# Attention scores of batches 1 to 7 as three fp32r products instead of one fp32 product

## The chip, the cores and the metric

The kernel runs on one core of one Trainium2 chip. Its time is the device time of one execution in microseconds; the figure for the kernel before is the median of three runs. The engines that matter here are TensorE (PE, with PEld for its weight loads), VectorE (DVE), ScalarE (ACT) and GpSimd (POOL). Each works through its own instructions in the order of the program and waits on semaphores that the others count up.

## The reference, cut to what matters

```python
x = x + attn(layernorm(x))          # x: 8 batches of 512 rows of 128
x = x + ffn(layernorm(x))           # 16 experts, the best 4 of each row
x = x + ssm(layernorm(x))
x = x + ffn(layernorm(x))

def attn(x):                        # one batch
    q, k, v = split(x @ w_qkv.T)
    scores = (q @ k.T) / sqrt(8)
    return softmax(scores) @ v @ w_proj.T + b_proj
```

The kernel folds the two projections of the scores into one matrix: `a_qk` is Wq^T Wk / sqrt(8), so with xn the normalised rows the scores are (xn a_qk) xn^T. What the kernel calls q is xn a_qk, and the other operand of the scores is xn itself.

## The kernel before

All four engines run an order that is written out by hand. The attention stage treats one batch per step, `step(i, ...)` for i from -1 to 7, and in step i three batches are in work at once: the softmax and output of batch i, the normalisation, the transposed rows `xnT` and the q of batch i+1, and the router (which experts a row goes to) of batches i-1 and i-2. Batch i has 512 rows, held as 4 groups r of 128 rows. The two sides of the buffers `xnT`, `qT` and `v` take turns by batch.

In a step from 2 to 6 the work goes round like this. Names in brackets are tiles, as the rows of the profile name them, with the line of the kernel before.

- PE: `scores(i, 0)`, `scores(i, 1)` (L1569), `router_turn(i-2)` (L1626, transposes of the router's rows `t0`), `scores(i, 2)`, `project(i-1)` (L1617), `scores(i, 3)`, `p_turn(i, 0)` and `p_turn(i, 1)` (L1599, transposes of the probabilities), `xn_turn(i+1)` (L1579), `router_logits`, `pv(i, 0)` (L1609), `q_proj(i+1)` (L1584), `p_turn(i, 2)`, `v_proj`, `p_turn(i, 3)`, the rest of `pv`, `router_parts`.
- ACT: `router_t` (L659 into tT, then L661 into ffn_hi), `exps(i, 0)` and `exps(i, 1)` (L623, probs), `pT` (L629), `xnT_out(i+1)` (L636), `exps(i, 2)`, `exps(i, 3)`, `q_out(i+1)` (L641), and later the rest of `pT`, `router_exp` (L666), `attn_out`, `v_out`.
- DVE: statistics of batch i+1 (L1050, L1053), `maxes(i, 0)` and `maxes(i, 1)` (L1065, neg_max), `xn_out(i+1)` (L1059), `maxes(i, 2)`, `x1_out` (L1075), the router's statistics of batch i-1 (L1081, L1084), `maxes(i, 3)`, the router's choice for batch i-2 (L1103 to L1140, of which L1128 waits for ACT's exponentials), and last `router_norm(i-1)` (L1090, four tensor_scalar instructions into t0) and `router_xn(i-1)` (L1096).
- POOL: `ln1_chain(i+1)` (L460, L462), `add_bias(i+1)` (L468), `router_stash(i-2)` (L454, the low part of the router's rows, a subtraction of 128x512), and `router_chain(i-1)` (L434 and L449, nine small instructions, each of which waits for the one before it). `router_norm(i-1)` on DVE waits for the ninth.

The score product of one group of rows in fp32 is one matmul in the program; the trace shows two records for it. The FFN stages that follow already hold their operands as a high part (a copy in fp32r) and a low part (the fp32 value less the high part), and form each product in three passes. After the last attention step POOL also splits the first rows of routing weights in step 7 (`rows_split`, L476 and L478), directly behind the router's chain of step 6.

Of the kernel before, what the change touches and what calls it, by code (L numbers as in the profile page):

```python
# [39 lines left out]
def build(nc, x, w_qkv, w_proj, b_proj, W_in, conv_w, conv_b, dt_bias, A_log, Dskip, norm_w, W_out,  # L40
          ffn_scale, gate_w, gate_b, mlp1_w, mlp1_b, mlp2_w, mlp2_b, out):
    with ExitStack() as ctx:
# [82 lines left out]
        with ExitStack() as stage:  # L125
            def own(name, shape, dt=F32):
                return stage.enter_context(nc.sbuf_tensor(name, shape, dt))


            w2_rows = own("w2_rows", [P, NE, I])  # L130
            w1_rows = own("w1_rows", [P, NE, D])
            xnT = own("xnT", [P, 2, SEQ])
            qT = own("qT", [P, 2, SEQ])
            probs = own("probs", [P, NT, SEQ])
            probsT = own("probsT", [P, NT, NT, P])
            v = own("v", [P, 2, NT, D])
            attn = own("attn", [P, NT, D])
            neg_max = own("neg_max", [P, NT])
            row_sum = own("row_sum", [P, NT])
            row_rec = own("row_rec", [P, NT])  # L140
            proj_rows = own("proj_rows", [P, D])
            qkv_rows = own("qkv_rows", [P, 3, D])

            tap_rows = w1_rows.rearrange("p (k w) d -> p k w d", w=CONV_W)
        with ExitStack() as stage:
# [42 lines left out]
        def bank(i):  # L188
            return ps[:, i, :]
# [29 lines left out]
        gate_b_all = vecs[:, VG:VG + NE]  # L219

        S1 = {n: sem("attn_" + n) for n in (
            "stats", "aggr", "rstd", "xn", "xnT_ps", "xnT", "q_ps", "q", "v_ps", "v", "scores", "max", "probs",
            "pT_ps", "pT", "o_ps", "rec", "o", "y_ps", "xb", "x1")}

        def router_sems(tag):
# [166 lines left out]
        def _(eng):  # L392
# [77 lines left out]

            eng.wait_ge(consts, N_CONST)

            def rows_split(F):
                b = 0
                wait(eng, rows_in, 48 * (b + done(F) + 1))
# [14 lines left out]
            def step(i, odd, first, second, third, fourth):  # L490
                if not first:
                    rows_split(F1)
                if first:
                    ln1_chain(i + 1)
                    add_bias(i + 1)
                if fourth:
                    router_stash(R1, i - 2)
                if third:
                    router_chain(R1, i - 1)
            skewed(eng, step, before={1: lambda: (late_constants(), ssm_weights()), 2: b2_parts})  # L500

            def ssm_norm(b):
# [104 lines left out]
        def _(eng):  # L607
# [30 lines left out]
            def q_out(b, par):  # L638
                wait(eng, S1["q_ps"], b + 1)
                wait(eng, S1["scores"], NT * (b - 1))  # L640
                eng.activation(qT[:, par, :], bank(4), ACT.Copy).then_inc(S1["q"], 1)  # L641

            def v_out(b, par):
                wait(eng, S1["v_ps"], b + 1)
# [205 lines left out]
            def step(i, odd, first, second, third, fourth):  # L850
# [26 lines left out]
                    pT(i, 1)  # L877
                if first:
                    xnT_out(i + 1, 1 - odd)
                if second:  # L880
                    exps(i, 2)
                if first:
# [160 lines left out]
        def _(eng):  # L1043
# [18 lines left out]
            def maxes(b, r):  # L1062
                wait(eng, S1["scores"], NT * b + r + 1)
                wait(eng, S1["probs"], NT * (b - 1) + r + 1)
                eng.tensor_reduce(neg_max[:, r:r + 1], bank(r), AX.X, ALU.max, negate=True).then_inc(S1["max"], 1)  # L1065

            def recip(b):
                wait(eng, S1["probs"], NT * b + NT)
# [296 lines left out]
            def step(i, odd, first, second, third, fourth):  # L1365
# [27 lines left out]
                    prep(i + 1, 3)  # L1393
                if fourth:
                    router_top(R1, i - 2)
                if second:
                    recip(i)
                if fourth:
# [151 lines left out]
        def _(eng):  # L1550
# [13 lines left out]
            def scores(b, par, r):  # L1564
                if (b, r) == (0, 0):
                    eng.wait_ge(prep_sb, 3)
                wait(eng, S1["q"], b + 1)
                wait(eng, S1["pT"], NT * (b - 1) + r + 1)
                eng.matmul(bank(r), qT[:, par, r * P:(r + 1) * P], xnT[:, par, :], start=True,  # L1569
                           stop=True).then_inc(S1["scores"], 1)  # L1570

            def xn_turn(b):
                if b:
                    wait(eng, S1["xn"], NT * b + NT)
                wait(eng, S1["q"], b)
                for r in range(NT):
                    if b == 0:
                        eng.wait_ge(S1["xn"], r + 1)
# [549 lines left out]
```

## Time and profile before

| | |
|---|---|
| median of three runs | 724.89 us (724.85 to 726.3) |
| the profiled execution, its own time | 726.56 us |
| span of the profiled execution | 724.8 us |
| PE busy over the span | 98% |
| DVE, ACT, POOL busy | 86%, 79%, 34% |
| attention steps 2 to 6, start of `scores(i, 0)` | 44.26, 57.57, 70.89, 84.20, 97.52 us |

The span is the time from the first to the last instruction that the profiler recorded. Busy shares are averages over stages; the change touches the attention stage alone, roughly the first 125 us.

### The profile page before, as it was taken

Reading aid. Unit: us, or ns where it says so; the run is one execution under the profiler, and the core shown is the slowest. Engines: PE = TensorE matmul, PEld = TensorE weight load, DVE = VectorE, ACT = ScalarE, POOL = GpSimd, SP = SyncE. Lnnn points to the kernel's source line nnn. Section 1 sums busy time; section 2 is a strip of 40 time slices with the busy share of each in tenths; the row PEclk is TensorE's granted clock in tenths of the full one; section 3 lists DMA queues with packets and bytes.
Section 4 is the critical chain, followed back from the end, with each engine's and each line's share of the span. In section 5 each row is a group of like instructions: output and inputs, shape, how many; then the busy total and the mean of one; then the engine's idle time right before and its main releaser. Section 6 shows DMA issues by size and latency. Waiting matters only on the chain.

```text
span 724.8 us, 13089 instructions
## 1 busy us (share of the span) xinstructions
PE 711.4 (98%) x3826; PEld 580.4 (80%) x3826; DVE 625.4 (86%) x1503; ACT 574.8 (79%) x1097; POOL 242.9 (34%) x389
## 2 busy tenths in 40 slices
PE   8999999999999999999999999999999999999998
PEld 6788787888788877778888888888878887887886
DVE  3678886999999999967689899899889989898996
ACT  2776767988988899778787787777678889888885
POOL 2454564000015100015757767767760000610000
PEclk9999999999999999999999999999999999999999
DMA  9000002654555454300000000000055455555651
GB/s 264 16 2 3 12 30 91 224 191 158 182 189 187 163 172 182 141 0 2 1 1 1 4 3 1 9 4 1 33 202 194 171 194 201 200 189 169 223 198 52
DMA packets 29380, 77.19 MB, mean 106 GB/s; under 512 B 4899, under 2 KB 9726, under 8 KB 29310
## 3 DMA queue, kind: packets, MB, share of 16 engines
q1 hardware_dynamic: 28980, 76.29, 30.9%
q8 instruction: 31, 0.51, 0.3%
q14 instruction: 39, 0.32, 0.1%
q10 hardware_dynamic: 330, 0.08, 0.0%
HBM read 73.73 MB, written 2.62 MB: 105 GB/s over the span
## 4 chain that ended last, share of the span: by engine, by line
PE 49%; DVE 2%; issue 1%; POOL 1%; ACT 1%; DVEq 0%; POOLq 0%; ACTq 0%
PE ps L1701 4%; PE ps L1703 4%; PE ps L1702 4%; PE ps L1733 4%; PE ps L1734 4%; PE ps L1735 4%; PE ps L1950 3%; PE ps L1755 3%; PE ps L1756 3%; PE ps L1757 3%; PE ps L1973 2%; PE ps L2008 2%; PE ps L1959 2%; PE ps L1985 1%; PE ps L1965 1%
## 5 line engine op out<-in xcount | busy, mean ns | idle before, releaser
L712 ACT ACTIVATE s_ring<-ps,b1T 128x512 f32<-128x512 f32 x256 | 171.3, 687 | 35.9 <-PE ps L1735 34.6
L1183 DVE SCALAR_TENSOR_TENSOR s_ring<-s_ring,top_col,r_all 128x1024 f32<-128x1024 f32 x128 | 166.3, 1300 | 19.2 <-ACT s_ring L712 18.4
L1195 DVE TENSOR_TENSOR s_lo<-s_ring,s_hi 128x1024 fp32r<-128x1024 f32 x126 | 153.6, 1219 | 1.9 <-ACT s_hi L718 1.9
L718 ACT ACTIVATE s_hi<-s_ring 128x1024 fp32r<-128x1024 f32 x128 | 135.0, 1055 | 9.9 <-DVE s_ring L1183 8.9
L1701 PE MATMUL ps<-s_hi,w_hi 128*128 128x512 f32 x256 | 101.7, 397 | 2.6 <-DVE s_lo L1195 2.5
L1733 PE MATMUL ps<-ffn_hi,w_hi 128*128 128x512 f32 x256 | 103.7, 405 | 0.2 <-ACT s_ring L712 0.2
L1703 PE MATMUL ps<-s_hi,w_lo 128*128 128x512 f32 x256 | 101.3, 396 | 0.0
L1735 PE MATMUL ps<-ffn_hi,w_lo 128*128 128x512 f32 x256 | 101.2, 395 | 0.0
L1734 PE MATMUL ps<-ffn_lo,w_hi 128*128 128x512 f32 x256 | 101.1, 395 | 0.0
L1702 PE MATMUL ps<-s_lo,w_hi 128*128 128x512 f32 x256 | 100.9, 394 | 0.0
L1701 PEld LDWEIGHTS ps<-s_hi,w_hi 128*128 128x128 f32 x256 | 48.2, 188 | 17.0 <-DVE s_lo L1195 6.2
L527 POOL TENSOR_TENSOR ramp<-upto,dt_a 128x512 f32<-128x512 f32 x32 | 33.0, 1041 | 85.4 <-PE ps L1703 73.8
L1702 PEld LDWEIGHTS ps<-s_lo,w_hi 128*128 128x128 f32 x256 | 48.2, 188 | 11.1
L1735 PEld LDWEIGHTS ps<-ffn_hi,w_lo 128*128 128x128 f32 x256 | 48.0, 188 | 11.3
L1703 PEld LDWEIGHTS ps<-s_hi,w_lo 128*128 128x128 f32 x256 | 48.2, 188 | 11.0
L1733 PEld LDWEIGHTS ps<-ffn_hi,w_hi 128*128 128x128 f32 x256 | 48.2, 188 | 10.7 <-ACT s_ring L712 0.7
L1734 PEld LDWEIGHTS ps<-ffn_lo,w_hi 128*128 128x128 f32 x256 | 48.2, 188 | 9.7
L454 POOL TENSOR_TENSOR ffn_lo<-tT,ffn_hi 128x512 fp32r<-128x512 f32 x16 | 22.5, 1404 | 88.8 <-ACT ffn_hi L661 88.8
L434 POOL TENSOR_TENSOR rt_small<-rt_small,mhalf 128x4 f32<-128x4 f32 x32 | 37.8, 1181 | 2.5
L1260 DVE SCALAR_TENSOR_TENSOR conv_acc<-ps,conv_taps,conv_acc 128x511 f32<-128x511 f32 (+2 forms) x48 | 35.0, 742 | 1.4 <-ACT conv_acc L769 1.3
L434 POOL TENSOR_TENSOR rt_small<-rt_mv,eps 128x4 f32<-128x4 f32 x16 | 7.7, 480 | 81.2 <-DVE rt_mv L1084 80.5
L1973 PEld LDWEIGHTS ps<-xb_tok,gram 128*128 128x128 f32 x256 | 32.9, 192 | 1.9 <-issue 0.5
(267 smaller groups left out, 1559.4 us busy)
## 6 DMA issues: line engine op xcount, KB each, us to landing
r_all<-route_dram SPq DMA_DIRECT2D x128, 512.0 KB, 3.9
out_dram<-X SPq DMA_DIRECT2D x7, 256.0 KB, 4.3
X<-in_L_attn_a_x_dram SPq DMA_DIRECT2D x1, 1536.0 KB, 8.6
rows_f<-route_dram SPq DMA_DIRECT2D x48, 32.0 KB, 3.0
w_rows<-in_L_ffn_mlp_w_dram SPq DMA_DIRECT2D x1, 1024.0 KB, 7.9
route_dram<-route_cols SPq DMA_DIRECT2D x64, 8.0 KB, 1.5
X<-in_L_attn_a_x_dram SPq DMA_DIRECT2D x2, 256.0 KB, 5.5
ssm_rows<-in_L_attn_b_W_in_dram SPq DMA_DIRECT2D x1, 384.0 KB
```

The lines of the kernel that those rows point to most:

```text
L434: eng.tensor_tensor(o, a, bb, op).then_inc(R["pool"], 1)
L712: eng.activation(s_ring[q % NR][:, e % 2, :], h_bank(F, b, e), ACT.Silu, bias=b1T[:, e:e + 1], scale=ALPHA).then_inc(F["act"], 1)
L718: eng.activation(s_hi[q % NR][:, :, :], s_ring[q % NR][:, :, :], ACT.Copy).then_inc(F["hi"], 1)
L1183: eng.scalar_tensor_tensor(out=s_ring[q % NR][:, :, :], in0=s_ring[q % NR][:, :, :], scalar=top_col[:, 0:1], in1=r_all[q % NR][:, :, :], o ...
L1195: eng.tensor_tensor(s_lo[q % NR][:, :, :], s_ring[q % NR][:, :, :], s_hi[q % NR][:, :, :].bitcast(F32), ALU.subtract).then_inc(F["lo"], 1)
L1701: eng.matmul(bank(6), w2_hi[:, e, :], hi, start=False, stop=False)
L1702: eng.matmul(bank(6), w2_hi[:, e, :], lo, start=False, stop=False)
L1703: mm = eng.matmul(bank(6), w2_lo[:, e, :], hi, start=False, stop=(e == NE - 1))
L1733: eng.matmul(h_bank(F, b, e), w1_hi[:, e, :], ffn_hi[:, b, :], start=True, stop=False)
L1734: eng.matmul(h_bank(F, b, e), w1_hi[:, e, :], ffn_lo[:, b, :], start=False, stop=False)
L1735: eng.matmul(h_bank(F, b, e), w1_lo[:, e, :], ffn_hi[:, b, :], start=False, stop=True).then_inc(F["h"], 1)
L1973: mm = eng.matmul(bank(3)[:, h * HD:(h + 1) * HD], gram[:, c % 2, h, :], xb_tok[:, c % 2, h // 2, (h % 2) * HD:(h % 2 + 1) * HD], start=Fa ...
```

## The change

From batch 1 on, the score product uses three fp32r passes: high q by high rows, low q by high rows, high q by low rows. Batch 0 keeps the fp32 product, with its q in a tile of its own. Four things are new in every step from 0 to 6, for batch i+1: on ACT `xnT_high` copies xnT into `xnT_hi`, between `xnT_out` and `exps(i, 2)`; on POOL `xnT_low` subtracts to get `xnT_lo`, between `add_bias` and the router's chain; on DVE `q_low` subtracts `qT` (now fp32r) from q's bank to get `qT_lo`, ahead of `recip`; and PE waits for the three of them. On POOL the two router pieces also change places: `router_chain` now stands ahead of `router_stash`.

```diff
-            qT = own("qT", [P, 2, SEQ])
+            qT = own("qT", [P, 2, SEQ], F32R)
...
+            xnT_hi = own("xnT_hi", [P, 2, SEQ], F32R)
+            xnT_lo = own("xnT_lo", [P, 2, SEQ], F32R)
+            qT_lo = own("qT_lo", [P, 2, SEQ], F32R)
+            q_first = own("q_first", [P, SEQ])
...
+            def xnT_low(b, par):
+                wait(eng, S1["xnT_hi"], b)
+                wait(eng, S1["scores"], NT * (b - 1))
+                eng.tensor_tensor(xnT_lo[:, par, :], xnT[:, par, :], xnT_hi[:, par, :].bitcast(F32),
+                                  ALU.subtract).then_inc(S1["xnT_lo"], 1)
...
                 if first:
                     ln1_chain(i + 1)
                     add_bias(i + 1)
+                if first and second:
+                    xnT_low(i + 1, 1 - odd)
+                if third:
+                    router_chain(R1, i - 1)
                 if fourth:
                     router_stash(R1, i - 2)
-                if third:
-                    router_chain(R1, i - 1)
...
-                eng.activation(qT[:, par, :], bank(4), ACT.Copy).then_inc(S1["q"], 1)
+                out = q_first[:, :] if b == 0 else qT[:, par, :]
+                eng.activation(out, bank(4), ACT.Copy).then_inc(S1["q"], 1)
+
+            def xnT_high(b, par):
+                wait(eng, S1["xnT"], b + 1)
+                wait(eng, S1["scores"], NT * (b - 1))
+                eng.activation(xnT_hi[:, par, :], xnT[:, par, :], ACT.Copy).then_inc(S1["xnT_hi"], 1)
...
                     xnT_out(i + 1, 1 - odd)
+                    xnT_high(i + 1, 1 - odd)
                 if second:
                     exps(i, 2)
...
+            def q_low(b, par):
+                wait(eng, S1["q"], b + 1)
+                wait(eng, S1["scores"], NT * (b - 1))
+                eng.tensor_tensor(qT_lo[:, par, :], bank(4), qT[:, par, :].bitcast(F32), ALU.subtract).then_inc(S1["q_lo"], 1)
...
                     router_top(R1, i - 2)
+                if first and second:
+                    q_low(i + 1, 1 - odd)
                 if second:
                     recip(i)
...
-                eng.matmul(bank(r), qT[:, par, r * P:(r + 1) * P], xnT[:, par, :], start=True,
-                           stop=True).then_inc(S1["scores"], 1)
+                rows = slice(r * P, (r + 1) * P)
+                if b == 0:
+                    eng.matmul(bank(r), q_first[:, rows], xnT[:, par, :], start=True,
+                               stop=True).then_inc(S1["scores"], 1)
+                    return
+                wait(eng, S1["xnT_hi"], b)
+                eng.matmul(bank(r), qT[:, par, rows], xnT_hi[:, par, :], start=True, stop=False)
+                wait(eng, S1["q_lo"], b)
+                eng.matmul(bank(r), qT_lo[:, par, rows], xnT_hi[:, par, :], start=False, stop=False)
+                wait(eng, S1["xnT_lo"], b)
+                eng.matmul(bank(r), qT[:, par, rows], xnT_lo[:, par, :], start=False, stop=True).then_inc(S1["scores"], 1)
```

POOL's rows in one step from 2 to 6, in the kernel before (`ln_ve` and `ln_rs` are the normalisation of the attention, `rt_small` is the router's chain, `ffn_lo` the stash):

```order
L460 TENSOR_TENSOR ln_ve<-ln_mv,eps 128x4
L462 TENSOR_TENSOR ln_rs<-ln_ve,mhalf 128x4
L468 TENSOR_TENSOR X<-X,vecs 128x512
L454 TENSOR_TENSOR ffn_lo<-tT,ffn_hi 128x512
L434 TENSOR_TENSOR rt_small<-rt_mv,eps 128x4
...
L434 TENSOR_TENSOR rt_small<-rt_small,ones 128x4
L449 TENSOR_TENSOR rt_small<-rt_small,rt_mv 128x4
```

The same step in the changed kernel:

```order
L464 TENSOR_TENSOR ln_ve<-ln_mv,eps 128x4
L466 TENSOR_TENSOR ln_rs<-ln_ve,mhalf 128x4
L472 TENSOR_TENSOR X<-X,vecs 128x512
L480 TENSOR_TENSOR xnT_lo<-xnT,xnT_hi 128x512
L438 TENSOR_TENSOR rt_small<-rt_mv,eps 128x4
...
L438 TENSOR_TENSOR rt_small<-rt_small,ones 128x4
L453 TENSOR_TENSOR rt_small<-rt_small,rt_mv 128x4
L458 TENSOR_TENSOR ffn_lo<-tT,ffn_hi 128x512
```

The new subtraction stands where the stash stood, and the stash now stands behind the ninth instruction of the chain.

ACT's rows from `router_t` to `q_out` in the same step, before:

```order
L659 ACTIVATE tT<-ps,scale_col 128x512
L661 ACTIVATE ffn_hi<-tT 128x512
L623 ACTIVATE probs,row_sum<-ps,neg_max 128x512 x2
L629 ACTIVATE probsT<-ps 128x512 x2
L636 ACTIVATE xnT<-ps 128x512
L623 ACTIVATE probs,row_sum<-ps,neg_max 128x512 x2
L641 ACTIVATE qT<-ps 128x512
```

And in the changed kernel:

```order
L677 ACTIVATE tT<-ps,scale_col 128x512
L679 ACTIVATE ffn_hi<-tT 128x512
L635 ACTIVATE probs,row_sum<-ps,neg_max 128x512 x2
L641 ACTIVATE probsT<-ps 128x512 x2
L648 ACTIVATE xnT<-ps 128x512
L659 ACTIVATE xnT_hi<-xnT 128x512
L635 ACTIVATE probs,row_sum<-ps,neg_max 128x512 x2
L654 ACTIVATE qT<-ps 128x512
```

One copy is added, between `xnT_out` and the third group's exponentials.

## Rows read from the trace of the kernel before

**Rows 1.** The page, part 1: busy time of each engine, share, instructions.

```profile
PE 711.4 (98%) x3826; PEld 580.4 (80%) x3826; DVE 625.4 (86%) x1503; ACT 574.8 (79%) x1097; POOL 242.9 (34%) x389
```

**Rows 2.** Busy time by stretch, step 5: length, engines, granted clock, DMA.

```profile
84.20:97.52 13.32, 13.32 (x94) 10.73 (x93) 11.25 (x56) 9.18 (x23) 7.20 (x13) 1.00 0.15 51
```

**Rows 3.** Timeline of PE, steps 5 and 6: start, length, what, count.

```profile
86.36 1.02 PE L1569 MATMUL ps<-xnT,qT 128*128 128x512 f32 x2
87.22 1.05 PE L1617 MATMUL ps<-vpg,attn 128*128 128x128 f32 x8
...
99.67 1.02 PE L1569 MATMUL ps<-xnT,qT 128*128 128x512 f32 x2
```

**Rows 4.** Timeline of PE, step 7: six fp32r passes between fp32 work.

```profile
118.31 0.48 PE L1733 MATMUL ps<-ffn_hi,w_hi 128*128 128x512 f32 x1
...
119.79 1.04 PE L1599 MATMUL ps<-ident,probs 128*128 128x128 f32 x8
```

**Rows 5.** Timeline of DVE, steps 4 and 5.

```profile
83.37 1.11 DVE L1090 TENSOR_SCALAR t<-X,rt_mv,rt_small 128x128 f32<-128x128 f32 x4
...
86.97 1.25 DVE L1065 TENSOR_REDUCE neg_max<-ps 128x1 f32<-128x512 f32 x2
...
92.22 0.66 DVE L1065 TENSOR_REDUCE neg_max<-ps 128x1 f32<-128x512 f32 x1
...
95.78 0.24 DVE L1128 TENSOR_TENSOR rt_tmp<-rt_tmp 128x64 f32<-128x64 f32 x1 [0.90 <-ACT rt_tmp L666]
```

**Rows 6.** Timeline of ACT, step 5.

```profile
86.56 0.69 ACT L659 ACTIVATE tT<-ps,scale_col 128x512 f32<-128x512 f32 x1 [0.42 <-PE ps L1626]
87.36 0.63 ACT L661 ACTIVATE ffn_hi<-tT 128x512 fp32r<-128x512 f32 x1
87.90 0.67 ACT L623 ACTIVATE probs<-ps,neg_max 128x512 f32<-128x512 f32 x1
...
89.61 1.08 ACT L629 ACTIVATE probsT<-ps 128x512 f32<-128x512 f32 x2 [0.28 <-PE ps L1599]
90.58 0.60 ACT L636 ACTIVATE xnT<-ps 128x512 f32<-128x512 f32 x1
```

**Rows 7.** Timeline of POOL, step 5.

```profile
89.74 1.28 POOL L468 TENSOR_TENSOR X<-X,vecs 128x512 f32<-128x512 f32 x1 [1.33 <-DVE xn L1059]
90.98 1.27 POOL L454 TENSOR_TENSOR ffn_lo<-tT,ffn_hi 128x512 fp32r<-128x512 f32 x1
92.38 0.20 POOL L434 TENSOR_TENSOR rt_small<-rt_mv,eps 128x4 f32<-128x4 f32 x1
...
96.30 0.20 POOL L449 TENSOR_TENSOR rt_small<-rt_small,rt_mv 128x4 f32<-128x4 f32 x1
```

**Rows 8.** Timeline of POOL, end of step 6 and start of step 7.

```profile
109.59 0.20 POOL L449 TENSOR_TENSOR rt_small<-rt_small,rt_mv 128x4 f32<-128x4 f32 x1
109.72 0.61 POOL L476 CAST rows_r<-rows_f 80x512 fp32r<-80x512 f32 x1
110.41 1.27 POOL L478 TENSOR_TENSOR rows_r<-rows_f,rows_r 16x512 fp32r<-16x512 f32 x1
114.90 1.27 POOL L454 TENSOR_TENSOR ffn_lo<-tT,ffn_hi 128x512 fp32r<-128x512 f32 x1 [3.22 <-ACT ffn_hi L661]
```

**Rows 9.** Timeline of DVE, end of step 6; the last row is instructions 2 to 4.

```profile
110.33 2.20 DVE L1090 TENSOR_SCALAR t<-X,rt_mv,rt_small 128x128 f32<-128x128 f32 x4
...
111.69 0.85 DVE L1090 TENSOR_SCALAR t<-X,rt_mv,rt_small 128x128 f32<-128x128 f32 x3
```

**Rows 10.** Timeline of ACT, start of step 7.

```profile
114.09 0.63 ACT L661 ACTIVATE ffn_hi<-tT 128x512 fp32r<-128x512 f32 x1
114.63 0.67 ACT L623 ACTIVATE probs<-ps,neg_max 128x512 f32<-128x512 f32 x1
```

**Rows 11.** Timelines of ACT and POOL, step 1.

```profile
37.21 0.60 ACT L636 ACTIVATE xnT<-ps 128x512 f32<-128x512 f32 x1
...
38.94 0.20 POOL L434 TENSOR_TENSOR rt_small<-rt_mv,eps 128x4 f32<-128x4 f32 x1 [3.07 <-DVE rt_mv L1084]
```

More of the change, by code:

```diff
@@ L221, in build @@
         S1 = {n: sem("attn_" + n) for n in (
-            "stats", "aggr", "rstd", "xn", "xnT_ps", "xnT", "q_ps", "q", "v_ps", "v", "scores", "max", "probs",
+            "stats", "aggr", "rstd", "xn", "xnT_ps", "xnT", "xnT_hi", "xnT_lo", "q_ps", "q", "q_lo", "v_ps", "v", "scores", "max", "probs",
             "pT_ps", "pT", "o_ps", "rec", "o", "y_ps", "xb", "x1")}
@@ L1575, in xn_turn @@
                 wait(eng, S1["q"], b)
+                wait(eng, S1["q_lo"], b - 1)
                 for r in range(NT):
```

## The prediction

> **What bounds the kernel now.** I read the page first: PE is busy 98% of the span, DVE 86%, ACT 79%, POOL 34% [rows 1]. Then the stretches: a step of the attention stage takes 13.32 us, PE is busy in all of it at a granted clock of 1.00, and DVE has 11.25 us of work, ACT 9.18, POOL 7.20 [rows 2]. The five steps from 2 to 6 start 13.31 us apart, and the timeline of PE shows the same place one step later at 99.67 - 86.36 = 13.31 us [rows 3]. So PE sets the step, and time taken from PE comes out of the end, as long as nothing else is nearly as late. That is the question here, since everything the change adds lies on the other three. The timelines of DVE, ACT and POOL [rows 5 to 7] show a ring that runs through them and closes once a step, almost as long as PE's step:
>
> `router_norm` (DVE, 83.37) - `router_xn` and the statistics - `maxes(i, 0)` (86.97) - `exps(i, 0)` (ACT, 87.90) - `pT` - `xnT_out` (90.58). On the other side `router_stats` - `router_chain` on POOL (92.38 to 96.30 + 0.20) - `router_norm` of the next step (83.37 + 13.31 = 96.68), 0.18 us after the chain's end. In the kernel before, the first half and the second touch only through DVE's own order. The change ties them: `xnT_low` waits for ACT's copy of `xnT_out`, and the router's chain stands behind `xnT_low`.
>
> **What PE gains.** One fp32 score product takes 87.22 - 86.36 = 0.86 us [rows 3]. Six fp32r passes of the same 512 columns between fp32 work take 119.79 - 118.31 = 1.48 us, so three take 0.74 [rows 4]. Four groups give back 4 x 0.12 = 0.48 us a step, and PE then has 12.8 us of work. The weight loads of fp32r stay hidden in that row.
>
> **The ring after the change.** I count from E, the start of `exps(i, 0)`.
>
> - `xnT_out` starts at 90.58 - 87.90 = 2.68 and lasts 0.60, to 3.28 [rows 6]. PE's transposes between them wait for ACT's probabilities, so an earlier PE does not pull this in.
> - `xnT_high` is new. Its twin is L661, the same copy of 128x512 to fp32r: it starts 87.36 - (86.56 + 0.69) = 0.11 after the copy it reads and lasts 0.63 [rows 6]. End 4.02.
> - ACT to POOL: L454 starts at 114.90, and the copy it waits for ended at 114.09 + 0.63 = 114.72, so 0.18 [rows 8, 10]. `xnT_low` starts at 4.20.
> - `xnT_low` is the twin of the stash, 1.27 us [rows 7]. After such an instruction the next starts 90.98 - 89.74 = 1.24 behind its start [rows 7]: the chain starts at 5.44. Before it started at 92.38 - 87.90 = 4.48, so this is 0.96 later.
> - From the chain's first start to its last 96.30 - 92.38 = 3.92 [rows 7]: 9.36.
> - The stash now follows at once. What follows the ninth instruction directly starts 109.72 - 109.59 = 0.13 later [rows 8], so it runs from 9.49 to 10.76, just when `router_norm` is released at about 9.6.
> - Here the trace shows something that the order alone doesn't. In step 6 `router_norm` starts at 110.33, POOL's 512-column subtraction L478 at 110.41, and the four instructions take 2.20 us where they take 1.11 in step 4; numbers 2 to 4 start at 111.69, when L478 ends (110.41 + 1.27 = 111.68) [rows 5, 8, 9]. So DVE's tensor_scalar is held until POOL's long instruction has ended, and then needs 0.85 more [rows 9]. For the stash that gives an end of `router_norm` at 10.76 + 0.85 = 11.61. Unheld it takes 1.11, so the rest of DVE runs as if it had started at 10.50.
> - `router_norm` to `maxes(i+1, 0)` is DVE's own work without a gap: 86.97 - 83.37 = 3.60 [rows 5]. The maximum takes 0.66, and ACT starts some 0.04 later [rows 5]: E of the next step is 10.50 + 4.30 = 14.80.
>
> The step becomes 14.80 us in place of 13.31, **1.49 us longer**. PE's 0.48 us is then worth nothing. Without the hold `router_norm` would start at 9.36 + 0.20 + 0.03 = 9.59 and the step would be 13.89, 0.58 longer. The same sum for the kernel before is 4.48 + 3.92 + 0.23 + 4.30 = 12.93, so the ring has 0.38 us of slack now.
>
> The Trainium skill bears on the hold: "GPSIMD Engine Reference", section 8, says that GpSimd shares its SBUF interfaces with VectorE and contends with VectorE instructions in a 2-port perf mode or with two SBUF inputs. "VectorE: DVE Perf Modes", on mode 2x_2P, puts tensor_scalar from SBUF to SBUF there, in fp32 too. By that rule the stash and `router_norm` collide in every step; with no such rule the sum would be the one without the hold. The trace agrees with the rule in the step 6 collision, 2.20 us against 1.11 [rows 5, 9].
>
> **What else is added.** `q_low` reads one bank and one SBUF tile, like `neg_max` over a bank, 0.66 us [rows 5]. It falls in the 0.90 us that DVE idles for the router's exponentials ahead of L1128 [rows 5]. If that cover were gone it would cost up to 0.66 a step, but with POOL's chain later than before it has another microsecond. It also delays `recip`, which only `attn_out` needs, at the end of the step. `xnT_high` pushes `exps(i, 2)` by some 0.6 us; `exps(i, 3)` waits for its maximum anyway. The stash, one chain later, is needed by `router_t` of the next step, and ends before it. `xnT_low` runs beside statistics and maxima, as the stash did. No DMA moves. Step 0 has no chain and POOL and ACT idle there, so I count nothing.
>
> **The sum.**
>
> - Step 1: `xnT_low` starts at 37.21 + 0.60 + 0.11 + 0.63 + 0.18 = 38.73, the chain at 39.97 instead of 38.94 [rows 11]: 1.03 later. ACT's start of `exps` is 87.90 - (86.97 + 0.70) = 0.23 behind DVE's path in step 5 [rows 5, 6]; I take 0.3 of slack. **+0.7**
> - Steps 2 to 5: 4 x 1.49 = **+6.0**
> - Step 6: before, the hold was there already: `router_norm` ended at 111.69 + 0.85 = 112.54, which is 11.33 after E (87.90 + 13.31 = 101.21) [rows 6, 9]. Now the stash stands ahead of the two pieces of `rows_split`: stash start 9.49, L476 at 10.73, L478 0.69 behind it at 11.42, its end 12.69, `router_norm` ends at 13.54 [rows 7, 8]. **+2.2**, and +0.3 if DVE gets its four through ahead of them. In step 6 before POOL won with an instruction that came 0.08 us later, so I take 2.2.
> - Step 7 and after: E follows `router_norm` as before, 114.63 - 112.54 [rows 9, 10]; the FFN, the SSM and the second FFN move as a block. The stash in step 7 has nothing hurried behind it. **0**
>
> Together **+8.9 us**. The profiled execution took 726.56 us at a span of 724.8; its sum gives 735.5. The median of the runs is 1.67 us lower, so there I expect 724.89 + 8.9 = **733.8 us**. The case's own range, from a step 0.1 us shorter or 0.15 longer and from +0.3 in step 6: 731.5 to 735.
>
> **Rivals.**
>
> - *The hold doesn't come* (0.14): if DVE, once released, gets ahead of the stash or runs between its accesses. Against it: the stash has started some 0.1 us earlier. Then 0.7 + 4 x 0.58 + about 0.6 = 3.6, so 728.5 us.
> - *PE stays the bound* (0.10, the other side): if `xnT_low` gets its data before the router's statistics are there, the chain is not late. The point at which that decides is 0.38 us of slack against 0.96 of delay, so my reading of one link would have to be off by over half a microsecond. Then six steps bring 0.48 us each, 2.9 in all: 722.0 us.
> - *More is held* (0.08): `xnT_low` or the later chain also hold DVE's small two-input instructions, or `q_low` lands on the ring. With 0.66 more a step in four to six steps: 736.5 to 738 us.
> - *The change shows nothing* (0.04): the gain and the delay meet, because the ring loses only its slack. 724.9 us.
> - *PE's clock falls* (0.02): PE would idle 2 us of a 14.8 us step, and the rows have no such stretch at a steady pace. With 12.8 of 14.8 us of work it stands a granted clock down to 0.87 without loss; below that the price is open.
>
> **The numbers.** My case has 0.62. What a measurement of this kernel can tell from no change is about 0.2%, 1.45 us. Slower by more: 0.62 + 0.14 + 0.08 + 0.02, less a little where the rivals are small, 0.85; faster 0.10; same 0.05. The range takes in my case and the one without the hold and a little of the worse: 727.8 to 736.
>
> **What would show it.** In the changed kernel: steps 2 to 5 some 14.8 us apart; PE idle twice, ahead of `router_turn` (waiting for DVE's t0) and ahead of `p_turn(i, 0)` (waiting for probs); the chain on POOL starting when `xnT_low` ends, about 5.4 us after `exps(i, 0)`; the four of `router_norm` at some 2.3 us in steps 2 to 5 and over 3 in step 6; a score group at 0.70 to 0.78 us. I am wrong if PE is still without gaps, if `router_norm` takes 1.1 us beside the stash, or if the chain starts at its old distance.

## The result and the profile after

| | before | after |
|---|---|---|
| median of the runs taken together | 725.6 us (724.85 to 726.74, 4 runs) | 732.6 us (732.28 to 733.58, 4 runs) |
| profiled execution, its own time | 726.56 us | 732.87 us |
| span | 724.8 us | 731.1 us |
| step 5, start of `exps(5, 0)` to that of the next step | 13.31 us | 14.62 us |

The ratio is 1.01, with a 95% interval of 1.0081 to 1.012: the change makes the kernel **slower by 7.0 us**. I had expected 733.8 us and a loss of 8.9.

The page of the kernel after, its first part (the same line as [rows 1]):

```profile
PE 709.2 (97%) x3854; PEld 582.6 (80%) x3854; DVE 635.2 (87%) x1510; ACT 580.5 (79%) x1104; POOL 250.4 (34%) x396
```

PE has 2.2 us less busy time although it has 28 more instructions, and the span is 6.3 us longer. So PE now waits. The busy time by stretch for step 5 of the kernel after (length, busy time of PE, PEld, DVE, ACT and POOL, granted clock, DMA share and rate):

```profile
85.90:100.53 14.63, 13.33 (x99) 11.29 (x97) 12.92 (x56) 10.04 (x24) 8.44 (x15) 1.00 0.15 47
```

PE was busy in all of step 5 before [rows 2]; now 1.30 us are missing. The clock is 1.00 in both, so it is no part of the loss. The first microseconds are another matter. Busy time from 8 to 14 us, in the profile of before and then in that of after:

```profile
8.00:14.00 6.00, 4.52 (x18) 3.02 (x17) 0.35 (x1) 2.09 (x4) 1.26 (x1) 0.72 0.95 344
```

```profile
8.00:14.00 6.00, 4.36 (x24) 2.99 (x25) 0.74 (x2) 3.07 (x6) 1.27 (x1) 1.00 1.02 344
```

The program is the same there. The granted clock was 0.72 in the execution of before, whose first score product began at 14.71 us, and 1.00 in the one of after, where it began at 13.08. The second execution thus enters the attention stage 1.63 us early for a reason outside the change, and so I compare distances between steps, not spans.

What the engines wait for in the stretch from 44 to 125 us of the kernel after (engine and line, who is waited for: us in total, times, longest):

```profile
PEld ps L1635 <- ACT probs L635: 9.1, 17, 1.4
ACT probs L635 <- DVE neg_max L1084: 7.3, 10, 1.0
POOL xnT_lo L480 <- ACT xnT_hi L659: 3.4, 5, 0.8
PE ps L1662 <- DVE t L1114: 3.0, 5, 1.8
DVE t L1114 <- POOL rt_small L453: 2.6, 5, 0.7
```

Read from the bottom up, this is the ring. DVE's `router_norm` (L1114) waits for POOL's chain (L453), POOL's `xnT_low` (L480) waits for ACT's copy (L659), ACT's exponentials wait for DVE's maxima, and PE, which no longer sets the pace, waits for ACT's probabilities and DVE's `t`. PE waits at the two places that I had named, once a step each. The timelines of PE, ACT, POOL and DVE in step 5 of the kernel after show it in order (start, length, what, count, and in brackets the idle time before it and what ended it):

```profile
87.82 0.66 PE L1662 MATMUL ps<-ident,t 128*128 128x128 f32 x4 [0.29 <-DVE t L1114]
91.78 1.32 PE L1635 MATMUL ps<-ident,probs 128*128 128x128 f32 x8 [1.00 <-ACT probs L635]
```

```profile
90.95 0.69 ACT L635 ACTIVATE probs<-ps,neg_max 128x512 f32<-128x512 f32 x1 [0.99 <-DVE neg_max L1084]
93.64 0.59 ACT L648 ACTIVATE xnT<-ps 128x512 f32<-128x512 f32 x1
94.26 0.63 ACT L659 ACTIVATE xnT_hi<-xnT 128x512 fp32r<-128x512 f32 x1
105.57 0.69 ACT L635 ACTIVATE probs<-ps,neg_max 128x512 f32<-128x512 f32 x1 [0.99 <-DVE neg_max L1084]
```

```profile
94.96 1.27 POOL L480 TENSOR_TENSOR xnT_lo<-xnT,xnT_hi 128x512 fp32r<-128x512 f32 x1 [0.65 <-ACT xnT_hi L659]
96.19 0.20 POOL L438 TENSOR_TENSOR rt_small<-rt_mv,eps 128x4 f32<-128x4 f32 x1
100.05 0.20 POOL L453 TENSOR_TENSOR rt_small<-rt_small,rt_mv 128x4 f32<-128x4 f32 x1
100.25 1.29 POOL L458 TENSOR_TENSOR ffn_lo<-tT,ffn_hi 128x512 fp32r<-128x512 f32 x1
```

```profile
99.59 0.22 DVE L1164 TENSOR_TENSOR rt_w<-rt_tmp,rt_sum 128x64 f32<-128x64 f32 x1
100.28 2.11 DVE L1114 TENSOR_SCALAR t<-X,rt_mv,rt_small 128x128 f32<-128x128 f32 x4 [0.47 <-POOL rt_small L453]
...
115.09 3.49 DVE L1114 TENSOR_SCALAR t<-X,rt_mv,rt_small 128x128 f32<-128x128 f32 x4 [0.65 <-POOL rt_small L453]
```

From `exps(5, 0)` at 90.95 the way goes to `xnT_out` at 93.64 (+2.69), the new copy at 94.26, the new subtraction at 94.96, the chain's first instruction at 96.19 and its ninth at 100.05. DVE is ready for `router_norm` at 99.81 and waits 0.47 us for that ninth. Its four instructions then take 2.11 us where they took 1.11 [rows 5], because the stash (100.25 to 101.54) starts 0.03 us ahead of them. The last DVE row is `router_norm` in step 6. The next `exps` starts at 105.57, which is 14.62 later.

### The profile page after: what moved, and what is told of

Same layout as the page of the kernel before. It is cut to its first block, busy times and chain, and to the rows that moved or that the text cites. A ratio compares the mean times of both kernels' runs of the same rounds, so it can differ in the third digit from the quotient of the medians.

```text
span 731.1 us, 13184 instructions
## 1 busy us (share of the span) xinstructions
PE 709.2 (97%) x3854; PEld 582.6 (80%) x3854; DVE 635.2 (87%) x1510; ACT 580.5 (79%) x1104; POOL 250.4 (34%) x396
## 4 chain that ended last, share of the span: by engine, by line
PE 43%; DVE 4%; issue 3%; POOL 3%; ACT 1%; DVEq 0%; POOLq 0%; ACTq 0%
PE ps L1986 3%; PE ps L1737 3%; PE ps L1739 3%; PE ps L1738 3%; PE ps L1791 3%; PE ps L1792 3%; PE ps L1769 3%; PE ps L1793 3%; PE ps L1770 3%; PE ps L1771 3%; PE ps L2009 2%; DVE s_lo L1219 2%; PE ps L2044 2%; PE ps L1995 2%; POOL rt_small L438 2%
```

## Experiments

Each kernel was timed against the kernel before; "+" is slower than before. Step lengths are distances of `exps(i, 0)` or `router_norm` in steps 3 to 5.

**1. The swap on POOL alone.** In the kernel before, only the order of the stash and the chain is exchanged.

```diff
-                if fourth:
-                    router_stash(R1, i - 2)
                 if third:
                     router_chain(R1, i - 1)
+                if fourth:
+                    router_stash(R1, i - 2)
```

> The kernel before with one thing of the change: on GpSimd the router's chain stands ahead of the stash. No split, scores in fp32. Ring and hold: the stash now runs just when the last of the router's choice (L1140) and router_norm want to run on VectorE, and holds one or both. Chain starts 4.48 us after exps(i, 0), as before; its end 8.6, stash 8.6 to 9.9, so the step goes from 13.31 to 13.9 (only router_norm held) or 14.25 (L1140 held too). In step 6 +1.3. Together +3.7 to +5.1 us over before. Rival, only the amount of added work counts: the swap adds none and TensorE stays without gaps, so 0 and a step of 13.31. Rival, the wait for xnT_lo alone makes the change slow: also 0 here.

Measured: 729.54 us against 724.88, ratio 1.0069 (1.0052 to 1.0086), **+4.7 us**. POOL and DVE in its step 4, from the timelines of this kernel:

```profile
84.75 0.20 POOL L449 TENSOR_TENSOR rt_small<-rt_small,rt_mv 128x4 f32<-128x4 f32 x1
84.96 1.27 POOL L454 TENSOR_TENSOR ffn_lo<-tT,ffn_hi 128x512 fp32r<-128x512 f32 x1
```

```profile
84.99 2.09 DVE L1090 TENSOR_SCALAR t<-X,rt_mv,rt_small 128x128 f32<-128x128 f32 x4
```

The stash starts 0.03 us ahead of `router_norm`, and the four take 2.09 us. No fp32r pass and no split is in this kernel, and two thirds of the whole loss are there. In step 2 the stash (from 56.21, 1.27 us) meets the instruction ahead of `router_norm` instead, the product of two 128x64 tiles at L1140: that one takes 1.26 us, and the four behind it take 1.10. The hold is thus shown by itself, and with it the place of a stash that nobody needs soon. Steps 4 and 5 are 14.13 and 14.14 us, where I had expected 13.9 for a hold of `router_norm` alone; the section after the experiments says where the missing 0.23 us lies.

**2. The stash taken out of the way, two ways.** In the changed kernel the order on POOL is stash, `xnT_low`, chain (2a), or stash, chain, `xnT_low` (2b, called low_last further down).

```diff
+                if fourth:
+                    router_stash(R1, i - 2)
                 if first and second:
                     xnT_low(i + 1, 1 - odd)
                 if third:
                     router_chain(R1, i - 1)
-                if fourth:
-                    router_stash(R1, i - 2)
```

> The changed kernel with the stash moved ahead of xnT_low: stash, xnT_low, chain. Nothing follows the chain, so nothing holds router_norm in steps 2 to 5; the price is a chain that starts some 0.56 us later. Ring and hold: step 14.2 in place of 14.62, and about 0.4 less in step 6, together 2.1 us less than the changed kernel. router_norm back to 1.1 us in steps 2 to 5. Rival, the ring without a hold (the four take long for a reason of their own): the later chain makes the step 0.56 longer, 15.2, and the kernel 3 us slower than the changed one.

Measured for 2a: 730.42 us, ratio 1.0077 (1.006 to 1.0094), 2.2 us less than the kernel after, by the medians. Its step is 14.17 us (75.14, 89.30, 103.47 us). `router_norm` in its step 4:

```profile
85.01 1.12 DVE L1114 TENSOR_SCALAR t<-X,rt_mv,rt_small 128x128 f32<-128x128 f32 x4 [1.01 <-POOL rt_small L453]
```

It is no longer held, 1.12 us, but it waits a full microsecond for the chain, which still stands behind `xnT_low`. This is not the wait for ACT's copy. That copy ends at 79.07 (78.44 + 0.63), and `xnT_low` starts at 79.68, directly behind the stash and with no wait for ACT in its row. That is 4.54 us after E (75.14) and not 4.01. The chain is late here because both long pieces stand ahead of it on POOL.

```profile
78.45 1.28 POOL L458 TENSOR_TENSOR ffn_lo<-tT,ffn_hi 128x512 fp32r<-128x512 f32 x1
79.68 1.28 POOL L480 TENSOR_TENSOR xnT_lo<-xnT,xnT_hi 128x512 fp32r<-128x512 f32 x1
```

```diff
-                if first and second:
-                    xnT_low(i + 1, 1 - odd)
-                if third:
-                    router_chain(R1, i - 1)
                 if fourth:
                     router_stash(R1, i - 2)
+                if third:
+                    router_chain(R1, i - 1)
+                if first and second:
+                    xnT_low(i + 1, 1 - odd)
```

> The changed kernel with xnT_low behind the router's chain: stash, chain, xnT_low. The chain no longer waits for ScalarE's copy and starts at about 4.6 us after exps(i, 0), but xnT_low now holds router_norm (from 8.7 to 10.0). Ring and hold: step 14.0, or 14.35 if L1140 is held too; 1.1 to 2.4 us less than the changed kernel over steps 2 to 5, and 0.6 to 1 less in step 1. Rival, no hold: step 13.1, bounded by the ring without the copy, 7 us less than the changed kernel.

Measured for 2b: 730.33 us, ratio 1.0073 (1.0056 to 1.009), step 14.17 to 14.19 us. The chain is early again, as before the change, and the time is that of 2a:

```profile
84.37 2.04 DVE L1114 TENSOR_SCALAR t<-X,rt_mv,rt_small 128x128 f32<-128x128 f32 x4
```

Now `xnT_low` stands where the stash stood in the kernel after, and holds `router_norm` in its place. So either of the two costs when it follows the chain directly, and in 2a, where neither does, the two cost as much by standing ahead of it.

**3. No low parts at all.** All three passes multiply the high parts, `xnT_low` and `q_low` are gone, POOL has its order of before; the copy `xnT_high` stays.

```diff
-                if first and second:
-                    xnT_low(i + 1, 1 - odd)
...
-                if first and second:
-                    q_low(i + 1, 1 - odd)
...
-                eng.matmul(bank(r), qT_lo[:, par, rows], xnT_hi[:, par, :], start=False, stop=False)
-                eng.matmul(bank(r), qT[:, par, rows], xnT_lo[:, par, :], start=False, stop=True)...
+                eng.matmul(bank(r), qT[:, par, rows], xnT_hi[:, par, :], start=False, stop=False)
+                eng.matmul(bank(r), qT[:, par, rows], xnT_hi[:, par, :], start=False, stop=True)...
```

> Leaves out both low parts: the three passes all read high q and high rows; no xnT_low, no q_low; GpSimd's order is that of before. ScalarE's copy xnT_high stays. So TensorE does what it does in the changed kernel, and GpSimd and VectorE what they did before. If the three passes give TensorE back 0.48 us a step, the step falls to between 12.83 (TensorE) and 13.05 (the ring, whose VectorE part waits for the router's exponentials): 1.6 to 2.9 us faster than before, 722.5 to 724. Rival, the passes themselves cost what they save (entry into fp32r, weight loads): no change against before, step 13.3.

Measured: 724.51 us, ratio 1.0003 (0.9992 to 1.0014). This **missed**: I expected a gain of 1.6 to 2.9 us and there is none. Steps 3 to 5 are 13.38, 13.17 and 13.26 us. The busy time of step 4 by stretch, and rows of the timelines of PE, DVE and POOL in that step:

```profile
72.51:85.68 13.17, 12.90 (x96) 11.16 (x95) 11.29 (x55) 10.04 (x24) 7.21 (x14) 1.00 0.02 4
```

```profile
73.34 1.33 PE L1628 MATMUL ps<-ident,probs 128*128 128x128 f32 x8 [0.26 <-ACT probs L633]
```

```profile
81.38 1.12 DVE L1112 TENSOR_SCALAR t<-X,rt_mv,rt_small 128x128 f32<-128x128 f32 x4
```

```profile
77.23 0.20 POOL L438 TENSOR_TENSOR rt_small<-rt_mv,eps 128x4 f32<-128x4 f32 x1
81.15 0.20 POOL L453 TENSOR_TENSOR rt_small<-rt_small,rt_mv 128x4 f32<-128x4 f32 x1
```

PE waits 0.26 us for the probabilities. `router_norm` is not held, but it starts 0.03 us after POOL's ninth instruction has ended (81.35), and so it does in step 3 (68.18 and 68.21) and in step 5 (94.61 and 94.64). (DVE's own list is done at about the same time in step 4, and earlier in steps 3 and 5.) So a ring through POOL sets this step too, and it is longer than the 12.93 us that I had worked out. It runs from `router_norm` of step 3 at 68.21 over DVE's statistics to the chain's start at 77.23, which is 9.02 us, then 3.92 to the ninth instruction and 0.23 to the next `router_norm`: 13.17. In the kernel before the first two distances are 92.38 - 83.37 = 9.01 and 3.92 [rows 5, 7]; with the same 0.23 behind them the ring is 13.16 us, so it had only 0.15 us of slack under PE's 13.31, and there was little for PE to give back under this order, with or without low parts. (The interval of the ratio reaches from 0.6 us faster to 1.0 slower, so the 0.04 us a step by which the three steps are on average shorter than 13.31 can't be seen in it.)

**4. The fp32 product again, with all that surrounds it.** The changed kernel, with all splits and places kept, but one fp32 product in the place of the three passes.

```diff
-            qT = own("qT", [P, 2, SEQ], F32R)
+            qT = own("qT", [P, 2, SEQ])
...
-                eng.matmul(bank(r), qT[:, par, rows], xnT_hi[:, par, :], start=True, stop=False)
                 wait(eng, S1["q_lo"], b)
-                eng.matmul(bank(r), qT_lo[:, par, rows], xnT_hi[:, par, :], start=False, stop=False)
                 wait(eng, S1["xnT_lo"], b)
-                eng.matmul(bank(r), qT[:, par, rows], xnT_lo[:, par, :], start=False, stop=True)...
+                eng.matmul(bank(r), qT[:, par, rows], xnT[:, par, :], start=True, stop=True)...
```

> The changed kernel with the scores as one fp32 product again; the three splits, their waits and GpSimd's order all stay (the low and high tiles are made and not used). If the ring sets the step, TensorE's 0.48 us a step are worth nothing in the changed kernel: step 14.62 as there, time within 0.5 us of it (732.6), with less idle time ahead of the transposes. Rival, TensorE's gain is real and part of the sum: 3 us slower than the changed kernel.

Measured: 733.32 us against 726.04, ratio 1.0102 (1.0087 to 1.0116), step 14.61 us. That is the kernel after to 0.01 us a step, and 7.3 us over its own kernel before where the kernel after is 7.0 over. PE's faster scores are worth nothing there, as predicted; the wait takes up what they save. PE in its step 5:

```profile
91.14 1.11 PE L1633 MATMUL ps<-ident,probs 128*128 128x128 f32 x6 [0.69 <-ACT probs L635]
```

The wait for the probabilities is 0.69 us, where with three passes it is 1.00. Beside experiment 1 this run also shows what the splits add: both have the fp32 product and the chain ahead of the stash, and the step is 14.61 us with the splits and 14.14 without, 0.47 more. The chain starts 5.25 us after `exps(4, 0)` (80.95 - 75.70) and not 4.72 (80.84 - 76.12), behind an `xnT_low` that waits 0.66 us for ACT's copy.

**5. DVE's work moved off the ring (stats_early).** To 2b I added that the statistics of the next batch (`ln1_stats`, L1069 and L1072) stand ahead of `router_norm`, where DVE would wait.

```diff
-                if first:
+                if first and i < 2:
                     ln1_stats(i + 1)
...
+                if third and i + 2 < NB:
+                    ln1_stats(i + 2)
```

> The order stash, chain, xnT_low (as in low_last), and on VectorE the statistics of batch i+2 moved from the start of step i+1 to the end of step i, ahead of router_norm. They read one SBUF input through one port, so xnT_low should not hold them: they run while it runs, and router_norm starts when it is done, at about 10.3 us after exps(i, 0), unheld, 1.1 us long. Behind it only router_xn stands ahead of the maxima. What is late next is ScalarE's path through t0, router_turn and its two copies, 2.1 us behind router_norm's end: step 13.5, against 14.17 in low_last; together 3 to 4 us less than low_last, 726 to 727. Rival, the statistics are held as well: step 14.2, no gain.

Measured: 730.95 us, ratio 1.0063 (1.0048 to 1.0077), step 14.03 us. **Missed**: I had expected 13.5. (The rows are those of the fastest of its six executions, 728.22 us; the others took 730.56 to 731.11.) DVE and POOL at the end of its step 4:

```profile
82.54 1.01 DVE L1164 TENSOR_TENSOR rt_w<-rt_tmp,rt_sum 128x64 f32<-128x64 f32 x1
83.47 0.86 DVE L1069 BATCH_NORM_STATS2 ln_st<-X 128x6 f32<-128x128 f32 x4
84.77 1.08 DVE L1114 TENSOR_SCALAR t<-X,rt_mv,rt_small 128x128 f32<-128x128 f32 x4
```

```profile
82.19 1.27 POOL L480 TENSOR_TENSOR xnT_lo<-xnT,xnT_hi 128x512 fp32r<-128x512 f32 x1
```

`router_norm` is free, but now `xnT_low` meets a small DVE instruction, the product of two 128x64 tiles at L1164. It takes 1.01 us where it took 0.22 in the kernel after, and ends when `xnT_low` does. That is the same collision as in step 2 of experiment 1. The hold had only moved.

**6. A shorter ring by other places.** To this I added that `exps(i, 0)` and `exps(i, 1)` stand ahead of `router_t` on ACT, and that DVE's `router_xn` waits until after `xn_out` of the next step.

```diff
-                if fourth:
-                    router_t(R1, i - 2, 7)
...
+                if fourth:
+                    router_t(R1, i - 2, 7)
...
+                if fourth:
+                    router_xn(R1, i - 2)
...
-                    router_xn(R1, i - 1)
```

> As stats_early, with two more moves that shorten the ring: ScalarE takes the exponentials of groups 0 and 1 ahead of the router's two copies, and router_xn goes behind xn_out of the next step. Then neither VectorE (maxima some 11.4 us after exps(i, 0)) nor ScalarE's router copies bound the step, and TensorE does, with 12.83 us of work and perhaps 0.3 of waiting for t0: step 12.9 to 13.2, 720.5 to 724, faster than the kernel before by 1 to 4 us. Rival, another path is just behind (VectorE's own work, 12.85 us a step with both new subtractions counted, or the later xnT): step 13.3 or more, no gain over before.

Measured: 731.39 us, ratio 1.0082 (1.0067 to 1.0097), step 14.43 us. **Missed** too, by over a microsecond a step. DVE and POOL in its step 4:

```profile
74.76 3.19 DVE L1120 TENSOR_SCALAR X<-X,rt_small 128x128 f32<-128x128 f32 x4
```

```profile
75.03 1.30 POOL L472 TENSOR_TENSOR X<-X,vecs 128x512 f32<-128x512 f32 x1 [2.03 <-DVE xn L1078]
76.28 1.33 POOL L458 TENSOR_TENSOR ffn_lo<-tT,ffn_hi 128x512 fp32r<-128x512 f32 x1
```

`router_xn` now stands beside `add_bias` and the stash, and takes 3.19 us for 1.11 of work. The first of its four instructions is done before `add_bias` starts; the second ends with `add_bias` (76.40 and 76.33), the third with the stash (77.70 and 77.61). Two misses of one kind said what to do: give each of POOL's three long pieces a place beside DVE work that it doesn't hold.

**7. Places that fit (the fitted kernel).** From the changed kernel: stash, then `xnT_low`, then the chain, as in 2a; statistics early, as in 5; `rows_split` at the end of step 7; and the second copy of `router_t` (now `router_hi`, into ffn_hi) behind `exps(i, 1)`.

```diff
-                if not first:
-                    rows_split(F1)
...
+                if fourth:
+                    router_stash(R1, i - 2)
                 if first and second:
                     xnT_low(i + 1, 1 - odd)
                 if third:
                     router_chain(R1, i - 1)
-                if fourth:
-                    router_stash(R1, i - 2)
+                if not first:
+                    rows_split(F1)
...
-                    router_t(R1, i - 2, 7)
+                    router_t(R1, i - 2, 7, 1)
...
+                if fourth:
+                    router_hi(R1, i - 2)
...
+                if third and i + 2 < NB:
+                    ln1_stats(i + 2)
```

> The three passes with everything that the runs so far speak for: on GpSimd stash, xnT_low, chain (nothing long behind the chain) and rows_split moved to the end of step 7; on VectorE the next statistics ahead of router_norm; on ScalarE the router's second copy behind exps(i, 1). router_norm then starts at about 10.1 us after exps(i, 0), unheld, and the ring closes at 10.1 + 2.3 + 0.7 = 13.1 us, TensorE's work is 12.8: step 13.1, 0.2 less than before. Step 1 still costs 0.7 and step 6 is about even: within 1 us of the kernel before, 724 to 726. Rival, the ring has another link that is late (xn_out, the copies pushed back): step 13.4 or more and 1 us or more slower than before. That it beats the kernel before by more than 1 us would need the step at TensorE's 12.8.

Measured: **723.57 us** against 725.0, ratio 0.9981 (0.997 to 0.9992), so 1.4 us faster than before and, by the two ratios, 8.6 us faster than the kernel after. POOL and DVE in its step 5:

```profile
87.17 1.28 POOL L472 TENSOR_TENSOR X<-X,vecs 128x512 f32<-128x512 f32 x1 [3.29 <-DVE xn L1084]
88.41 1.28 POOL L458 TENSOR_TENSOR ffn_lo<-tT,ffn_hi 128x512 fp32r<-128x512 f32 x1
89.63 1.28 POOL L480 TENSOR_TENSOR xnT_lo<-xnT,xnT_hi 128x512 fp32r<-128x512 f32 x1
```

```profile
88.33 0.87 DVE L1111 BATCH_NORM_STATS2 rt_st<-X 128x6 f32<-128x128 f32 x4
...
95.47 1.09 DVE L1120 TENSOR_SCALAR t<-X,rt_mv,rt_small 128x128 f32<-128x128 f32 x4
```

The three long pieces run back to back from 87.17 to 90.91, beside maxima, the addition from a bank and statistics, none of which is stretched. The chain ends at 94.93, 0.54 us before DVE comes to `router_norm`. The busy time of this step is below; the step is 13.05 us, as expected (13.1), and PE is busy in all but 0.02 of it:

```profile
84.06:97.11 13.05, 13.03 (x98) 11.37 (x97) 11.71 (x56) 9.71 (x24) 8.35 (x14) 1.00 0.17 52
```

The time came out better than the 724 to 726 that I expected, and not for the reason that I gave: I had put +0.7 us on step 1 and nothing on step 6. By the starts of `exps(i, 0)`, step 1 costs nothing (15.15 us for 15.13 before), step 2 costs 0.14, steps 3 to 5 gain 0.26 each, and step 6 gains 0.84 (12.58 for 13.42), 1.45 us in all. `router_norm` in its step 6:

```profile
108.02 1.12 DVE L1120 TENSOR_SCALAR t<-X,rt_mv,rt_small 128x128 f32<-128x128 f32 x4 [0.72 <-POOL rt_small L453]
```

It took 2.20 us there before [rows 9], beside `rows_split`, which now stands elsewhere. So more than half of the gain over the kernel before lies in step 6.

**8. Is it the passes or the order?** The fitted kernel with the fp32 product, by the same edit as in 4.

> The fitted order once more, with the fp32 score product in place of the three passes; all splits, copies and waits stay where they are. Theory 1: in the fitted order PE sets the step (no idle row of PE in steps 3 to 5), and the three passes are what brings it from 13.31 to 13.05 us. A step's four score groups are 3.04 us as passes (0.78, 0.70, 0.78, 0.78) and 4 x 0.86 = 3.44 us in fp32, and 0.17 us of PE's waiting for router_norm goes into the difference: step 13.05 + 0.40 - 0.17 = 13.28 us, 1.2 us in all above the fitted kernel, so the time is that of before or up to 0.5 us less, ratio 0.999 to 1.001. Theory 2: a ring of the other engines sets the 13.05 us, or the new order alone brings the gain: step 13.05 us, ratio 0.997 to 0.999 again.

Measured: 725.81 us against 724.83, ratio 1.0018 (1.0007 to 1.0029), which is above the 0.999 to 1.001 of theory 1. The four of `router_norm` in its steps 3 and 5, and the busy time of one step:

```profile
69.69 1.08 DVE L1120 TENSOR_SCALAR t<-X,rt_mv,rt_small 128x128 f32<-128x128 f32 x4
96.24 1.09 DVE L1120 TENSOR_SCALAR t<-X,rt_mv,rt_small 128x128 f32<-128x128 f32 x4
```

```profile
84.60:97.88 13.28, 13.28 (x94) 10.73 (x92) 11.74 (x56) 9.81 (x24) 8.37 (x14) 1.00 0.15 51
```

The step is 13.28 us, which is what theory 1 gave, and PE is busy in all of it. So in the fitted order the three passes do bring time: 13.28 to 13.05, 0.23 us a step. PE's work falls by 0.40; the other 0.17 is a wait of the fitted kernel for `router_norm`, whose transposes start at 96.61, 0.40 us after the pass ahead of them (96.21), where a next pass follows after 0.23. With step 2 (13.77 to 13.45) and step 6 (12.79 to 12.58) that makes 1.2 us over five steps, and the spans of the two profiles, 722.9 and 721.9 us, differ by 1.0. The ratios lie 0.0037 apart, which is 2.7 us, and their intervals allow 1.1 to 4.3. Where more than the 1.2 us would come from, the traces don't say. And since step 6 is 12.79 us here, 0.63 of the 0.84 us gained in that step come with the order and not with the passes; on the other side, step 2 is 0.46 us longer than in the kernel before.

## Why the prediction was right

**That the ring takes over: right.** The tie that I had named, `xnT_low` waiting for ACT's copy with the chain behind it, is in the trace as a wait of 0.65 us on POOL in step 5, and of 3.4 us in five steps. Experiments 1 and 4 differ by the splits, and these add 0.47 us a step. How much of that is the wait for ACT's copy and how much POOL's added subtraction, no run separates. Experiment 2a can't, since its `xnT_low` doesn't wait for ACT. Its step is POOL's row of work: `xnT_low` at E + 4.54, 1.24 to the chain, 3.85 to the ninth instruction, 0.24 to `router_norm` and 4.30 to the next `exps` make 14.17. The 13.89 of my forecast for a step without the hold is for the order of the changed kernel, and no run had that without the hold.

**The slack before the change: wrong.** My sum for the kernel before, 12.93 us, joined two distances that don't meet. The 4.48 to the chain's start counts from `exps(i, 0)`, which starts 0.23 us behind DVE's path, as I had noted myself under step 1, and the 4.30 is DVE's path without these 0.23. Counted from `router_norm` to `router_norm` the ring is 13.16 us and the slack 0.15, not 0.38. Experiment 3 has its 13.17 in step 4, and experiment 1 is this ring and the hold: 13.16 + 0.98 = 14.14. In the changed kernel ACT does wait for DVE (0.99 us), so the 14.80 doesn't contain this error.

**That the stash holds `router_norm`: right, and its size too.** I put 10.76 + 0.85 from E for its end. The trace has 11.44, exactly 0.85 behind the stash's end at 10.59. Experiment 1 gives the hold apart from all else. The rule of the Trainium skill ("GPSIMD Engine Reference", section 8) under which the two collide in every step is what happened: the trace agrees, with 2.11 us for 1.11 in the steady steps and 3.49 in step 6.

**That PE's gain is worth nothing in the changed kernel: right**, by experiment 4. Its size was wrong, and I should have read it from more rows. Six passes in 1.48 us [rows 4] hide that the first pass after fp32 work takes longer. In step 5 of the kernel after (start, length):

```profile
85.90 0.48 PE L1601 MATMUL ps<-xnT_hi,qT 128*128 128x512 f32 x1
...
86.68 0.39 PE L1601 MATMUL ps<-xnT_hi,qT 128*128 128x512 f32 x1
...
88.24 0.48 PE L1601 MATMUL ps<-xnT_hi,qT 128*128 128x512 f32 x1
...
89.02 1.05 PE L1653 MATMUL ps<-vpg,attn 128*128 128x128 f32 x8
```

A group that follows fp32 work takes 88.24 to 89.02, 0.78 us. Three of a step's four do, and only the second follows another group, at 0.70 us. The gain is 3.44 - 3.04 = 0.40 us a step, not 0.48.

**The sizes.** The term "steps 2 to 5" was 4 x 1.49 and measured 4 x 1.31 = 5.2 us. The 0.18 that is missing in each lies in four links. The copy starts 0.03 us behind what it reads where its twin gave 0.11 (and is 0.08 earlier at its end). ACT to POOL takes 0.07 and not 0.18. The chain takes 3.86 from first start to last, not 3.92. These bring the last operation to 9.10 where I had 9.36, and the stash takes 0.07 of it back, since it starts 0.20 behind the ninth instruction and not 0.13. Each was a single row of a neighbouring pair, and a start read from such a row may hold some other instruction's queue. Step 1 was +0.7 predicted and +0.74 measured. Step 6 was +2.2 and measured 15.10 - 13.42 = +1.7. The stash starts 9.49 us after E there (115.06 - 105.57), as forecast, and the last piece of `rows_split` ends at 12.66, forecast 12.69. What was wrong is the 0.85 us from there to the end of `router_norm`, which took three of the four instructions to be still to come:

```profile
115.09 1.89 DVE L1114 TENSOR_SCALAR t<-X,rt_mv,rt_small 128x128 f32<-128x128 f32 x2 [0.65 <-POOL rt_small L453]
116.91 1.67 DVE L1114 TENSOR_SCALAR t<-X,rt_mv,rt_small 128x128 f32<-128x128 f32 x2
```

```profile
116.29 0.61 POOL L486 CAST rows_r<-rows_f 80x512 fp32r<-80x512 f32 x1
116.98 1.25 POOL L488 TENSOR_TENSOR rows_r<-rows_f,rows_r 16x512 fp32r<-16x512 f32 x1
```

Each of POOL's three pieces holds one of DVE's four. The first ends with the stash, the second at 116.98 with the cast (116.90), the third with the subtraction (118.23), and only the fourth is left: the end comes 0.35 us later, 13.01 us after E and not 13.54. The FFNs and the SSM behind it move as a block: from `exps(7, 0)` to the end it is 610.4 us, before 610.2.

**The range of my case: luck.** I gave 731.5 to 735 us for it. The terms named there, 0.1 us shorter or 0.15 longer in each of four steps and +0.3 in step 6, give 733.4 to 734.7. The measured 732.6 lies below these; nothing in the prediction carries the 731.5, so that it fell inside is luck. The sum was 1.2 us too high by the trace, 0.7 in steps 2 to 5 and 0.5 in step 6.

**The sum against the medians.** Like for like the trace has lost 7.7 us by `exps(7, 0)`, and the medians differ by 7.0. The runs of before alone scatter by 1.9 us, 724.85 to 726.74, about what the 1.63 us of the first microseconds come to, so I leave that difference open.

**The rivals.** "The hold doesn't come" and "PE stays the bound" are out by experiments 1 and 4. "PE's clock falls" is out too: the granted clock is 1.00 in every step of the kernel after. "More is held" did not happen in the changed kernel, but its mechanism exists: experiment 5, and step 2 of experiment 1, show the small product held.

## What to carry to other kernels

Before a piece of work is put on an idle engine, write down what stands beside it on the others for its whole length: here POOL was idle for two thirds of the time, and yet a 1.3 us subtraction of POOL cost a microsecond of DVE's wherever it met a tensor_scalar or a product of two SBUF tiles, and nothing beside maxima, statistics and bank reads. (The router's statistics of step 3 took 1.08 to 1.09 us for 0.87 in the kernel before and in experiments 1 and 3; why is open.) An engine at 100% is worth speeding up only by the slack of the next ring, and there may be several; work out each around the whole step, from one instruction back to the same one, so that no part is left out between two sums. A change that loses 1.3 us a step can still hold a gain of 0.2, which the places of its pieces hide.

## What the runs showed of the hardware

- **A held DVE instruction ends with POOL's, not at half speed, and each long piece holds one.** Beside one long POOL instruction the first of DVE's four runs until that has ended, then the rest run as always: 1.11 us become 2.04 to 2.11. Beside several in a row one of the four ends with each: 3.19 us beside two (experiment 6), 3.49 beside three (stash and the two pieces of `rows_split`, step 6). A 128x64 product became 1.01 us from 0.22 in experiment 5, and 1.26 in experiment 1.
- **Small POOL instructions hold nothing.** In experiment 7 `router_norm` takes 1.09 us (95.47 to 96.56) beside two 128x4 instructions of POOL that start at 95.64 and 95.92, one of them 1.01 us long.
- **Going into fp32r costs.** The first pass after fp32 work takes 0.31 to 0.32 us to its successor's start, the next ones 0.23 to 0.24.
- **The first microseconds vary.** From 8 to 14 us the granted clock was 0.72 in the one profile and 1.00 in the other, on the same work of PE, and its first score product came 1.63 us later in the one than in the other.
